# Moving a statistics hand-over through DRAM from SyncE's queue to GpSimd's, in stage 1 of a transformer block kernel

## The reference, cut to what matters

```python
tp = (silu(time_emb) @ Wt + bt)[:, None, :]
shift_msa, scale_msa, gate_msa, shift_mlp, scale_mlp, gate_mlp = jnp.split(tp, 6, axis=-1)
mu  = jnp.mean(x, axis=-1, keepdims=True)           # per token
var = jnp.var(x, axis=-1, keepdims=True)
h = (x - mu) * rsqrt(var + eps) * g1 + be1
h = h * (1.0 + scale_msa) + shift_msa
qkv = h @ Wqkv + bqkv                               # then attention, MLP, second norm
```

## Time and profile before

| | |
|---|---|
| Median of 3 runs | 3798.04 us (3796.79 to 3798.82) |
| Profiled execution, span from its first to its last instruction | 3796.5 us |
| Profiled execution, own time beside the span | no separate figure is given; it is taken as its span, 1.5 us below the median |
| TensorE busy, over the span | 99% |
| VectorE, ScalarE, GpSimd busy | 64%, 48%, 53% |

### The profile page before, as it was taken

The page is one execution under the profiler, slowest core; times in us unless marked ns, Lnnn a source line. Parts: engine busy times, 40 slices in busy tenths (PEclk is TensorE's granted clock), DMA queues, the critical chain, the costliest instruction groups (busy, mean ns, idle before and its releaser), DMA issues.

```text
span 3796.5 us, 49838 instructions
## 1 busy us (share of the span) xinstructions
PE 3756.9 (99%) x18430; PEld 2612.0 (69%) x18430; DVE 2434.0 (64%) x4053; ACT 1806.3 (48%) x3222; POOL 2017.1 (53%) x685
## 2 busy tenths in 40 slices
PE   8899999999999999999999999999999999999998
PEld 6688885455555555555555555888888888888887
DVE  5577668888888888888888884343334444344443
ACT  3222225666666666666666666433333333333333
POOL 1000006989999999999999997322222222222221
PEclk9999999999999999999999999999999999999999
DMA  8677875667766776777677664111111111111110
GB/s 296 225 243 238 260 239 135 146 131 159 167 148 156 159 162 142 160 161 160 142 160 161 156 146 142 62 39 48 40 54 47 53 45 37 45 37 45 37 45 23
DMA packets 219001, 479.38 MB, mean 126 GB/s; under 512 B 22808, under 2 KB 61720, under 8 KB 202632
## 3 DMA queue, kind: packets, MB, share of 16 engines
q1 hardware_dynamic: 200616, 344.08, 31.5%
q0 software_dynamic: 18144, 132.13, 16.9%
HBM read 225.36 MB, written 117.60 MB: 90 GB/s over the span
## 4 chain that ended last, share of the span: by engine, by line
PE 88%; DVE 6%; DMA 3%; issue 1%; ACT 1%; POOL 0%; SPq 0%; DVEq 0%; POOLq 0%; ACTq 0%
PE psum L1235 13%; PE psum L679 13%; PE psum L1249 13%; PE psum L577 8%; PE psum L578 8%; PE psum L579 8%; PE psum L1890 6%; PE psum L1886 6%; PE psum L1888 6%; PE psum L1276 4%; PE psum L1262 1%; DVE max_part L1058 1%; DVE qk_out L1113 1%; DMA spread<-token_stats 1%; DMA token_stats<-packed 1%
## 5 line engine op out<-in xcount | busy, mean ns | idle before, releaser
L1058 DVE TENSOR_REDUCE max_part<-psum 128x1 f32<-128x512 f32 x2048 | 1262.7, 683 | 125.8 <-PE psum L679 113.9
L1491 POOL TENSOR_TENSOR probs_round<-probs_round,probs_round 128x2048 f32<-128x2048 f32 x189 | 888.2, 4699 | 29.7 <-PE psum L1249 24.7
L679 PE MATMUL psum<-k_stack,q_stack 96*128 96x512 f32 x2048 | 776.4, 408 | 5.1 <-DVE max_part L1058 1.5
L2055 DVE TENSOR_TENSOR g_parts<-g_full,g_parts 128x512 fp32r<-128x512 f32 x256 | 268.1, 1047 | 796.9 <-ACT g_parts L1944 796.9
L1235 PE MATMUL psum<-q_stack,k_stack 98*128 98x512 f32 x2048 | 774.9, 414 | 0.8 <-ACT probs_round L1369 0.5
L1369 ACT ACTIVATE probs_round<-psum 128x512 f32<-128x512 f32 x1024 | 543.3, 611 | 386.5 <-PE psum L1235 386.4
L1369 ACT ACTIVATE probs<-psum 128x512 f32<-128x512 f32 x1024 | 551.9, 598 | 154.4 <-PE psum L1235 117.9
L1491 POOL TENSOR_TENSOR probs_round<-probs_round,probs 128x2048 f32<-128x2048 f32 x124 | 568.6, 4586 | 9.7
L1940 ACT ACTIVATE g_full<-psum,cols 128x512 f32<-128x512 f32 x256 | 176.6, 690 | 802.7 <-PE psum L579 802.4
L1235 PEld LDWEIGHTS psum<-q_stack,k_stack 98*128 98x128 f32 x2048 | 379.3, 190 | 240.7 <-ACT probs_round L1369 67.4
L2151 POOL TENSOR_TENSOR y_out<-y_out,rows 128x512 f32<-128x512 f32 x60 | 77.1, 1285 | 859.0 <-DVE y_out L2090 859.0
(11 more groups left out here) (186 smaller groups left out, 4966.3 us busy)
## 6 DMA issues: line engine op xcount, KB each, us to landing
probs<-probs POOLq DMA_DIRECT2D x126, 1024.0 KB, 8.3
qk_parts<-qk_out SPq DMA_DIRECT2D x128, 512.0 KB, 4.5
k_stack<-qk_parts SPq DMA_DIRECT2D x96, 512.0 KB, 6.7
q_stack<-qk_parts SPq DMA_DIRECT2D x192, 256.0 KB, 5.4
v_rows<-v_out SPq DMA_DIRECT2D x64, 256.0 KB, 3.9
v_group<-v_rows SPq DMA_DIRECT2D x32, 512.0 KB, 10.6
gated_attention<-gated SPq DMA_DIRECT2D x64, 256.0 KB, 2.9
x<-in_x SPq DMA_DIRECT2D x16, 1024.0 KB, 9.4
```

The source lines that it names most:

```text
L679: pe.matmul(psum[:, SMAX[at.turn % 3], :], q_stack[u % 3][0:PARTS, h, i * P:(i + 1) * P], k_stack[G % 2][0:PARTS, h, kh * CH:(kh + 1) * CH ...
L1058: dve.reduce_max(max_part[:, n:n + 1], psum[:, SMAX[at.turn % 3], :], AX.X).then_inc(dve_smax, 1)
L1491: pool.tensor_tensor(total[:, :, :], total[:, :, :], probs(u, kt)[:, :, :], ALU.add).then_inc(pool_sum, 1)
```

## The change

Both DMAs of the hand-over, with their waits, go from SyncE's list to GpSimd's. For chunks 1 to 5 they stand behind the eighth subtraction (L1151) and ahead of the two memsets; for chunks 6 to 15 ahead of the `k_stack` memset. They have the same shapes, buffers and semaphores as before.

```diff
-            store_stats(sp, 1)
-            load_stats(sp, 1)
             for c in range(NC):
...
-                    if c + 2 < NC and i == 0:
-                        store_stats(sp, c + 2)
-                    elif c + 2 < NC and i == 2:
-                        load_stats(sp, c + 2)
...
-        def store_stats(sp, c):
-            sp.wait_ge(dve_mean, c)
-            sp.wait_ge(act_sqrt1, c + 1)
-            sp.dma_start(stat_dram[c].rearrange("(v p t) -> p v t", v=2, t=TT),
-                         packed[:, :, :]).then_inc(a_stat, 16)
-
-        def load_stats(sp, c):
-            sp.wait_ge(a_stat, 16 * c)
+        def pool_stats(pool, c):
+            pool.wait_ge(dve_mean, c)
+            pool.wait_ge(act_sqrt1, c + 1)
+            pool.dma_start(stat_dram[c].rearrange("(v p t) -> p v t", v=2, t=TT),
+                           packed[:, :, :]).then_inc(a_stat, 16)
+            pool.wait_ge(a_stat, 16 * c)
             if c >= 2:
-                sp.wait_ge(dve_full, c * KD)
-            sp.dma_start(spread[:, :], stat_dram[c].partition_broadcast(P)).then_inc(a_spread, 16)
+                pool.wait_ge(dve_full, c * KD)
+            pool.dma_start(spread[:, :], stat_dram[c].partition_broadcast(P)).then_inc(a_spread, 16)
...
+            for c in range(1, 6):
+                pool_stats(pool, c)
             pool.wait_ge(side_free, 4)
...
             pool.memset(ones_sq[:, :], 1.0).then_inc(pool_const, 1)
 
+            for c in range(6, NC):
+                pool_stats(pool, c)
             pool.wait_ge(side_free, 8)
```

## The result

The changed kernel takes **3827.18 us** (median of 5 runs, 3822.38 to 3829.97) against 3798.04 us: ratio 1.0073 (95% interval 1.0061 to 1.0085), 29 us slower. The forecast was 3796.2 us with a range to 3806, so it was wrong in its sign and in its range. The profiled execution has a span of 3825.2 us, 28.7 more than before.

What follows compares the result with a forecast made beforehand. VectorE follows its statistics loop through DRAM, TensorE its matmuls, at nearly the same pace with a cushion between. 3796.5 - 2.8 (early chunks) + 1.0 (chunks 3 to 10) = 3794.7; median 1.5 above: 3796.2 us, range 3791 to 3806.

Steps and rivals of the forecast that it cites:

- the cushion: Time from V0's eviction to the tile needing its bank: 1.54 us in chunk 5, 0.48 in chunk 10; hides longer hand-overs.
- The loop: Chunks 4 to 9: VectorE's loop through the hand-over becomes 0.5 us longer per chunk, from -0.2 to 2.3.
- Shares the DMA engines with them: Spread load, no longer ahead of Q/K stores and x loads in one queue: 0 to 0.8 us more, 0.3 taken.
- The store, +0.5: Statistics' store in each loop: +0.5 us for later first bytes from GpSimd, +0.3 to +1.4; the load likewise +0.5.
- What no longer waits, -0.8: Statistics' store in each loop: no longer issued behind V0's store on SyncE, which gives back 0.8 us.
- The 16-byte runs: Statistics' store from GpSimd: its 256 runs may double the 0.88 us issue, an upper end of +1.4 us.
- SyncE's removed wait: SyncE's wait for `a_stat` ahead of V3's store: removal costed at nothing, 0.3 us per chunk if it counted.
- Chunk 1: Store passes SyncE's full queue in perhaps 3 us; the 5.73 us stall shrinks to 2.7; -2.8 us arrives at 143 us.
- Start: First hand-over, behind the eighth subtraction: VectorE's slices start 1.7 us late (0 to 3), vanishing in the 5.73 us stall.
- The clock: Behind the shortened stall at 109 us the granted clock stays at 1.00 instead of 0.50, worth 1.5 us.
- The slow-descriptor case: GpSimd's pair adds 2.3 us or more to each loop; at 3 us, 3812 us; decides from 1.6; chance 0.13.
- VectorE holds GpSimd's port: During the load's issue a VectorE fp32 operation blocks GpSimd; loop 1.0 us longer, sum 3799.2 us; chance 0.15.

Runs made afterwards that it cites:

- without chunk 1's pair: The changed kernel, but the statistics' store and spread load of chunk 1 go from SyncE again: 1.0051, repeated at 1.0049, against the kernel before.
- the quiet run: Both DMAs on GpSimd, chunk 1's on SyncE; SyncE holds each chunk's first Q/K store and x load until the spread load has landed: 1.0029 against the kernel before.
- The version on ScalarE: Kernel before, with both DMAs of chunks 2 to 15 issued from ScalarE's list, chunk 1's from SyncE: 0.9991, repeated at 0.9992.
- the store alone: Kernel before, with only the statistics' store of chunks 2 to 15 moved to GpSimd, spread load and chunk 1 with SyncE: 1.0003.
- the run with all of it quiet: Both DMAs on GpSimd, chunk 1's on SyncE; SyncE holds V1's and all later stores and loads until the spread load has landed: 1.0054 against the kernel before.

## Why the prediction was wrong

**What bounds the kernel: right.** The loop of VectorE through DRAM, the cushion of about 2 us and "free until the cushion is gone and then its full excess" give TensorE's added idle time once the excess is known: 6 x 3.7 - 2 = 20 us against 18.4 measured, and 14.4 against 12.9 without chunk 1's pair. That the whole kernel without the pair is 20 us slower is another sum, with the early chunks and the clock in it. VectorE's own part of the loop is 24.1 us, not about 20. Both signs named for wrong came: statistics' stores of 4.0 to 4.4 us in five of six quiet chunks, and TensorE waiting for evictions from chunk 5 on. Nothing came from chunk 11 on, as written, and the memsets cost nothing that a row shows.

**The loop: the step that failed.** Its +0.5 us was 0.5 + 0.5 - 0.8 + 0.3, and it measured +3.7.
- *"Shares the DMA engines with them: 0 to 0.8 us more, I take 0.3"* is the term that was mis-sized. I read the load's new place as a share of bandwidth. It is an order: from GpSimd the load is issued only when a longer store has landed, and in five of six chunks 768 KB of SyncE's transfers are queued by then; where they were not, those behind the load held it up as well. With the 0.5 for GpSimd's own cost I had 0.8 us for the load; it takes 2.3 us longer, of which the quiet run gives GpSimd 0.3 at its start and nothing at its landing.
- *The store, +0.5,* measured +1.4, most of it from V1's and V2's stores, which stood behind it before. I had no term for them.
- *What no longer waits, -0.8:* the issue came 0.25 us earlier. GpSimd starts 0.48 us behind `packed`, and 0.29 us behind the landed store, where SyncE's second issue had followed at once: +0.27 for which the sum has no term.
- *+0.5 for the first bytes* was more than measured: 1.2 us in quiet against 0.9, +0.3. *The 16-byte runs* did not double the issue: 0.72 us against 0.88.

**SyncE's removed wait "at nothing".** Alone it was right: putting it back won nothing. But I had asked only what stood *behind* the wait (V3's store), and not what the two DMAs had been *ahead* of.

**Chunk 1: failed.** The -2.8 us rested on the small store passing the full queue. It took, in the chain of waits,

```profile
94.16 6.99 DMA token_stats<-packed
```

against 7.10 us. On ScalarE's queue it took 5.6 us there in one execution and 7.0 in the other. For GpSimd's queue the trace does not bear out what I drew from the rule of the Trainium skill ("DMA: Bandwidth & Descriptors", "Queues, rings and completion order"), that engines take turns between queues packet by packet; the sum without it, 2.8 us higher, was the better one. The stall behind it became 6.08 us instead of 2.7.

**Start: right in kind, wrong in what became of it.** The GpSimd timeline, start and length:

```profile
36.36 0.58 POOL L462 DMA_DIRECT2D spread<-token_stats  x1 [1.51 <-DMA token_stats<-packed]
```

The store was issued at 33.94 and landed at 36.06; 33.9 and 36.0 had been written. The load behind it took 7.3 us instead of 5.7. The slice then came at 43.77, not at 41.7, late by 3.7 us instead of 1.7. It was to vanish in the stall at 109 us; but VectorE, late too, sets that stall's end, so it moved along. Alone this cost about 3 us, not clear of no change, and within the change 5.

**The clock.** I expected a shorter stall to keep the clock. There was none; behind the stalls of 3.61 and 5.36 us it was 0.50, where behind the 3.40 us stall of before it had stayed at 1.00. In chunk 3 the stall is only 0.2 us longer, so 2.5 of its 2.75 us are slower matmuls; in chunk 10 TensorE is idle 5.9 us more, so 2.3 of the 8.2 us are. But chunk 3's part is not shown to come from the change. The version on ScalarE has both cases in two executions of one kernel, at 0.50 behind a stall of 3.62 us and at 1.00 behind one of 3.51:

```profile
141.50:146.00 4.50, 4.31 (x10) 3.44 (x11) 2.37 (x5) 0.69 (x1) 0.00 (x0) 0.50 0.80 215
143.50:148.00 4.50, 4.37 (x19) 3.64 (x20) 2.20 (x5) 1.38 (x2) 0.00 (x0) 1.00 0.82 204
```

Their chunk 3 takes 39.1 and 36.5 us. The low clock stands behind this stall in 14 of the 17 profiled executions, those of the store alone and of the ScalarE version among them; that it does not in the one profiled execution of the kernel before may be chance.

**The rivals.** The slow-descriptor case had the right sign, its 1.6 us for the tipping point, and at 3 us a loop 3812 us (by its own terms 3796.5 + 16 + 1.5 = 3814); its mechanism was wrong. Of all cases it came nearest, with a chance of 0.13, and the range stopped at 3806, inside it: no case let both DMAs meet traffic. *VectorE holds GpSimd's port* does not explain the loss: of the six loads of chunks 4 to 9 only that at 254.46, the shortest of them, has such an fp32 operation from SBUF to SBUF near its issue, 0.67 us behind its start. In the run with all of it quiet one load is issued just as such an operation starts:

```profile
290.92 0.48 DVE L1003 TENSOR_SCALAR wq_tmp<-wq_tmp,small 128x512 f32<-128x512 f32 x1
290.92 0.60 POOL L475 DMA_DIRECT2D spread<-token_stats  x1 [2.43 <-DMA token_stats<-packed]
```

Its issue took 0.60 instead of 0.55 us and it landed in 4.0, like the others. What "SBUF — State Buffer" of the Trainium skill describes (the "DVE blocks DMA" trap) is seen here in those 0.05 us at most.

**Open:** why the store lands near 2.2 us in some chunks and in 3.4 to 4.5 in others with the same stores beside it; whether the load is held up by transfers behind it on GpSimd's queue alone or on any second queue, since no run puts ScalarE's load in the same place (one of ScalarE's, with V3's store 0.24 us behind it, took 4.4 us, GpSimd's two with V3's store that close 5.4, a hint and no more); what makes the clock fall behind one stall of 3.5 us and not behind another; and whether the version on ScalarE is faster by 2 to 3 us.

## What to carry to other kernels

A queue is also an order: a DMA that is moved to another engine's queue is no longer ahead of what the first engine issues behind it. Before pricing such a move, list what the old queue issues in the 10 us behind the moved DMA, in bytes, and what kept that back; a wait put back in the old queue was no substitute here. And parts of a loop that are cheap alone (1 and 10 us) can cost more than their sum together (20 us): a cushion hides them only once, and here one part also made the other longer.

## What the runs showed of the hardware

- A load on GpSimd's queue got next to nothing beside a full SyncE queue: 2 packets against 478 in 2.8 us. In the next 4.0 us it moved 142. The queues' lines for 292.7 to 296.7 us:

```profile
q0 software_dynamic: 142, 0.52, 54.1%
q1 hardware_dynamic: 325, 0.62, 41.5%
```

- A 4 KB store to DRAM from GpSimd took 2.2 us (median) with V1's and V2's stores held back and 4.1 us with them beside it. In chunk 1's traffic the same store took 7.0 us from GpSimd and 7.1 from SyncE.
- GpSimd begins an issue 0.48 us behind another engine's work and 0.29 us behind a landed DMA, SyncE 0.02 us behind a landed one. GpSimd is busy for 0.55 us with the load's issue and 0.72 with the store's, where SyncE took 0.32 and 0.38.
